# Second gather stage of a graph network: three tiles of each pair picked by TensorE, one comparison per five node blocks, targets loaded as a spread bf16 row

## The reference

```python
# layer 0: per relation r, sum of norm * h[src] into dst, times W_r = sum_b w_comp[r,b] weight[b]
x = layernorm(x + relu(segment_sum(...) @ W + h_bias + x @ loop_weight))
# layer 1, on the new x
e = (x[dst] - x[src]) @ theta.T + x[src] @ phi.T
e = relu(batchnorm(e, g0, b0))       # statistics over all edges
e = relu(batchnorm(e @ fc1.T, g1, b1))
x = layernorm(x + relu(segment_mean(e, dst) + x))
```

## Time and profile before

| what | us |
|---|---|
| median of three runs | 2537.24 |
| the profiled execution | 2537.5 |
| its span | 2535.7 |
| TensorE matmul busy | 2051.7 |
| GpSimd busy | 1562.5 |
| VectorE busy | 1546.1 |
| ScalarE busy | 652.8 |

### The profile page before, as it was taken

The page is one execution under the profiler, slowest core; times in us unless marked ns, Lnnn a source line. Parts: engine busy times, 40 slices in busy tenths (PEclk is TensorE's granted clock), DMA queues, the critical chain, the costliest instruction groups (busy, mean ns, idle before and its releaser), DMA issues. The chain is left out here.

```text
span 2535.7 us, 49004 instructions
## 1 busy us (share of the span) xinstructions
PE 2051.7 (81%) x13488; PEld 1691.6 (67%) x13489; DVE 1546.1 (61%) x4106; ACT 652.8 (26%) x1087; POOL 1562.5 (62%) x1715
## 2 busy tenths in 40 slices
PE   4777777777677677689888888988988998999996
PEld 3766666666667667546666666666665444999995
DVE  5443433434433344787867767777776787777776
ACT  3211111111111112541111111111111774444444
POOL 6777777777777775477777777777777001940002
PEclk9988888888888888759889989988988999999998
DMA  4222222222222221553434333343343993344442
GB/s 108 73 65 72 70 67 72 64 72 64 74 71 64 71 60 41 175 177 116 134 114 134 115 124 125 115 133 117 114 134 111 329 303 129 131 141 146 146 149 84
DMA packets 129354, 291.65 MB, mean 115 GB/s; under 512 B 34541, under 2 KB 83478, under 8 KB 111492
## 3 DMA queue, kind: packets, MB, share of 16 engines
q1 hardware_dynamic: 72532, 139.41, 17.1%
q0 software_dynamic: 48640, 99.61, 15.2%
q10 hardware_dynamic: 8112, 51.91, 5.2%
HBM read 227.59 MB, written 63.21 MB: 115 GB/s over the span
## 5 line engine op out<-in xcount | busy, mean ns | idle before, releaser
L759 POOL DMA_INDIRECT G<-in_x,srcT x782 | 744.3, 952 | 246.2 <-issue 180.4
L774 POOL DMA_INDIRECT G<-btab,srcT x738 | 696.3, 943 | 268.9 <-issue 167.6
L858 PE MATMUL PS<-BIG,G 128*128 128x192 f32 x1564 | 354.6, 379 | 258.6 <-PEq L36 257.6
L858 PEld LDWEIGHTS PS<-BIG,G 128*128 128x128 f32 x1564 | 297.2, 220 | 289.9 <-issue 289.4
L1145 ACT ACTIVATE BIG<-PS 128x768 f32<-128x768 f32 x196 | 158.5, 809 | 785.0 <-ACTq L36 784.6
L1460 DVE TENSOR_TENSOR ACC<-ACC,PS 128x24 f32 x782 | 140.8, 180 | 318.6 <-DVEq L36 228.1
L869 PE MATMUL PS<-BIG 128*128 128x192 f32 (+1 forms) x1584 | 329.5, 370 | 0.5 <-PEq L36 0.5
L869 PEld LDWEIGHTS PS<-BIG 128*128 128x128 f32 x1584 | 318.5, 227 | 0.6 <-issue 0.6
L987 PE MATMUL PS<-BIG,ACC 128*128 128x256 bf16 x2112 | 286.9, 297 | 24.8 <-PEq L36 24.7
L987 PEld LDWEIGHTS PS<-BIG,ACC 128*128 128x128 bf16 x2112 | 215.3, 106 | 96.1 <-issue 54.9
L1234 ACT ACTIVATE BIG<-PS 128x512 f32<-128x512 f32 x174 | 103.7, 596 | 594.4 <-ACTq L36 588.8
(11 more groups left out here) (208 smaller groups left out, 2347.6 us busy)
## 6 DMA issues: line engine op xcount, KB each, us to landing
BIG<-spill SPq DMA_DIRECT2D x90, 1024.0 KB, 4.9
spill<-BIG ACTq DMA_DIRECT2D x49, 1024.0 KB
G<-in_x,srcT POOLq DMA_INDIRECT x782
typ_i<-in_edge_type SPq DMA_DIRECT2D x97, 128.0 KB
G<-btab,srcT POOLq DMA_INDIRECT x738
BIG<-atab SPq DMA_DIRECT2D x196, 60.0 KB
atab<-BIG SPq DMA_DIRECT2D x12, 384.0 KB, 2.9
xn<-in_x SPq DMA_DIRECT2D x48, 64.0 KB
```

What stands on the lines that cost most here:

```text
L759: nc.gpsimd.indirect_dma_start(out=G[0:n, g % 2, t, :], out_offset=None, in_=x, in_offset=bass.IndirectOffsetOnAxis(ap=srcT[0:n, TPG * g + ...
L774: nc.gpsimd.indirect_dma_start(out=G[0:n, g % 2, t, :], out_offset=None, in_=btab[:, :], in_offset=bass.IndirectOffsetOnAxis(ap=srcT[0:n, ...
L858: mm = pe.matmul(PS[:, 2 * c + q // 2, (q % 2) * ZW:(q % 2 + 1) * ZW], G[:, h, TPC * k + q, :], soh[:, p, TPC * c + q, :, :].rearrange("p ...
```

## The change

- `PICK` becomes three tiles, so a pair has 29 gathers. The picking matmuls have 384 columns.
- The codes are written five times, the j-th lowered by j, so that one comparison with 5b makes the one-hots of the five blocks 5b to 5b+4 (`BATCH = 5`, ten batches, the last with four used blocks). The batches move: the first is made and used at chunk 0 of the pair.
- TensorE's spreading of picks and ScalarE's codes move ahead of chunk 0's own work on their engines.
- The targets are stored once in setup as bf16 rows in DRAM (`rel_d`, and as float32 in `relf_d` for chunks that span more than one window), and SyncE loads each group's row spread over 80 partitions. The spreading matmuls L973 go, and the look-up compares in SBUF. Its wait for the one-hot buffer (`cnt_done`) now stands in front of it.
- Four PSUM banks instead of two hold the chunks in work (`e_free` 4). The last chunk of a pair is copied in two activations.

```diff
-    PICK = 2 * TILE
-    PICK_Q = TPC - 2
+    PICK = 3 * TILE
+    PICK_Q = TPC - 3
-    PICK_ROW, PICK_COLS, PICK_STEP = 3, 86, 88
-    BATCH = 7
+    PICK_ROW, PICK_COLS, PICK_STEP = 3, TILE, TILE + 2
+    BATCH = 5
+    NBATCH = 10
...
-            return {1: (0,), 2: (1,), 3: (2,), 4: (3,), 5: (4,), 6: (5, 6)}.get(at_c, ())
+            return {0: (0,), 1: (1, 2), 2: (3,), 3: (4, 5), 4: (6,), 5: (7, 8), 6: (9,)}.get(at_c, ())
...
                 take(sp, dig_free)
-                sp.dma_start(digits[:, h, :], digits_d[:, bass.ds(g * GROUP, GROUP)]).then_inc(dig_in[h], 16)
+                row = rel_d[bass.ds(g * CPG, CPG), :].rearrange("(o k) n -> o (k n)", o=1).to_broadcast([WIN, CPG * REL_CHUNK])
+                sp.dma_start(rel[:, h, :, :].rearrange("p k n -> p (k n)"), row).then_inc(dig_in[h], 16)
...
                     for k in range(CPG):
                         if wide_chunks:
                             reach = reach_of(pe, CPG * g + k)
+                        if picking(g, h, use) and h == 0 and k == 0:
+                            spread_picks()
                         reached(pe, "pe", b_gathered[CPG * h + k], b_landed(g, h, use, k))
...
-                        nxt = after(g, h, use, k)
-                        nxt = nxt and after(*nxt)
-                        if nxt:
-                            spread_dst(*nxt)
...
             def code_picks():
                 take(act, pick_spread_done)
                 act.sem_inc(pick_rows_free, 1)
-                full = PICK // PICK_COLS
-                act.activation(pick_code[:, 0:full, 0:PICK_COLS], pick_spread[:, 0:full * PICK_COLS].rearrange("p (r c) -> p r c", r=full),
-                               ACT.Identity, bias=small[:, 62:63])
-                act.activation(pick_code[:, full, 0:PICK - full * PICK_COLS], pick_spread[:, full * PICK_COLS:PICK],
-                               ACT.Identity, bias=small[:, 62:63]).then_inc(pick_code_ready, 1)
+                for j in range(BATCH):
+                    ins = act.activation(pick_code[:, j, :, 0:PICK_COLS], pick_spread.rearrange("p (r c) -> p r c", r=PICK_ROW),
+                                         ACT.Identity, bias=pick_bias[:, j:j + 1])
+                ins.then_inc(pick_code_ready, 1)
...
                     if u is not None:
                         unit_high_part(u)
+                    if picking(g, h, use) and h == 0 and k == 0:
+                        code_picks()
                     take(act, look_done)
...
                     if u is not None:
                         unit_mid_part(u)
-                    if picking(g, h, use) and h == 0 and k == 0:
-                        code_picks()
                 act.sem_inc(dig_free, 1)
...
-            def look_up(k):
-                take(dve, d_ready)
-                dve.tensor_scalar(ohT[0:WIN, k % 2, :], PS[0:WIN, k % 2, :], node_col[0:WIN, 0:1], None, ALU.is_equal).then_inc(ohT_ready, 1)
+            def look_up(g, h, use, k):
+                if k == 0:
+                    reached(dve, "dve", dig_in[h], 16 * (use + 1))
+                dve.tensor_scalar(ohT[0:WIN, k % 2, 0:CHUNK + 1].rearrange("p (r n) -> p r n", r=REL_ROW),
+                                  rel[:, h, k, :].rearrange("p (r n) -> p r n", r=REL_ROW)[:, :, 0:REL_COLS],
+                                  node_col[0:WIN, 0:1], None, ALU.is_equal).then_inc(ohT_ready, 1)
...
-                for w in range(BATCH * b, BATCH * (b + 1)):
-                    ins = dve.tensor_scalar(pick_oh[:, BATCH * (b % 2) + w % BATCH, :].rearrange("p (r c) -> p r c", r=PICK_ROW),
-                                            pick_code[:, :, 0:PICK_COLS], float(w), None, ALU.is_equal)
-                ins.then_inc(pick_oh_ready, 1)
+                take(dve, pick_oh_free)
+                dve.tensor_scalar(pick_oh[:, BATCH * (b % 2):BATCH * (b % 2 + 1), :].rearrange("p j (r c) -> p (j r) c", r=PICK_ROW),
+                                  pick_code[:, :, :, 0:PICK_COLS].rearrange("p j r c -> p (j r) c"), float(BATCH * b), None,
+                                  ALU.is_equal).then_inc(pick_oh_ready, 1)
```

More of the change, by code:

```diff
@@ L197, in gnn_kernel @@
         awx = part(3 * D // 2).bitcast(BF16).rearrange("p (a d) -> p a d", a=3)
+        relx = part(CHUNK)[0:WIN, :]
+        pick_hi, pick_rows = (part(PICK // 2).bitcast(BF16) for _ in range(2))
         at[0] = 2 * GROUP + CPG * CHUNK + GROUP
@@ L236, in gnn_kernel @@
         f_hi, f_lo, f_dst, f_min = (rows(accf, k) for k in range(4))
-        i_rel, i_hi = (rows(accf, k, I32) for k in range(4, 6))
+        i_hi = rows(accf, 5, I32)
         a_hi = i_hi
-        dig_hi, dig_lo = (bst[0:NR, k, :].bitcast(BF16).rearrange("p (b e) -> p b e", b=TPR) for k in range(2))
+        rel_rows_b = flat(bst[:, :, :])[0:NR, 0:TPR // TPC * REL_CHUNK // 2].bitcast(BF16).rearrange("p (c r n) -> p c r n", c=TPR // TPC, r=REL_ROW)
         t_min, t_max, t_first, t_reach, t_ext = (part(TPR)[0:NR, :] for _ in range(5))
@@ L670, in store_picks @@
                 sp.wait_ge(picks_ready, 1)
-                for k, dg in enumerate((pick_lo64, pick_hi)):
+                for k, dg in enumerate((pick_lo, pick_hi)):
                     sp.dma_start(picks_d[k, :, :], dg[0:ODD, :]).then_inc(rows_out, 16)
@@ L984, in pick_rows_of @@
                 take(pe, pick_oh_ready)
-                for w in range(BATCH * b, BATCH * (b + 1)):
+                for w in range(BATCH * b, min(BATCH * (b + 1), NW)):
                     for a in range(3):
-                        mm = pe.matmul(picked, table_part(w, a), pick_oh[:, BATCH * (b % 2) + w % BATCH, 0:PICK],
+                        mm = pe.matmul(picked, table_part(w, a), pick_oh[:, BATCH * (b % 2) + w % BATCH, :],
                                        start=(w == 0 and a == 0), stop=False, skip_group_check=True)
@@ L1137, in copy_z @@
             def copy_z(g, h, use):
+                if isinstance(g, int) and g == 1:
+                    act.wait_ge(rows_out, 16 * 6)
                 for k in range(CPG):
@@ L1233, in store_e @@
                     else:
-                        act.activation(to, PS[:, 2 + k % 2, :], ACT.Copy).then_inc(act_self, 1)
+                        act.activation(to, PS[:, k, :], ACT.Copy).then_inc(act_self, 1)
                         take(act, act_self)
@@ L1604, in count_hots @@
                 tiles = bass.ds(TPG * g + TPC * k, TPC)
-                take(dve, cnt_done)
                 dve.tensor_tensor(oh_lo[:, k % 2, :, :], over(steps_lo, TPC, TNODES), each(loT[:, tiles], TNODES), ALU.is_equal)
@@ L1681, in one @@
                         if nxt:
-                            look_up(nxt[3])
+                            take(dve, cnt_done)
+                            look_up(*nxt)
                             count_hots(nxt[0], nxt[3])
                         u = unit_of(g, k)
-                        if u is not None:
-                            unit_rest_part(u)
                         if isinstance(g, int) and (g, k) == (1, 1):
@@ L1701, in one @@
                             dve.sem_inc(look_done, 1)
+                        if u is not None:
+                            unit_rest_part(u)
                         if k >= 1:
@@ L1712, in edge_features @@
                 by_pairs(dve, NG, one, head=FIRST_PICK, tail=HELD // 2)
-            look_up(0)
+            look_up(0, 0, 0, 0)
+            take(dve, cnt_done)
             count_hots(0, 0)
```

71 lines of the change are left out of this document (33 added, 38 removed).

## The result

| | before | after |
|---|---|---|
| median, us | 2537.32 (6 runs, 2535.61 to 2538.57) | 2615.45 (6 runs, 2613.41 to 2616.12) |
| ratio to before | | 1.0306 (95%: 1.0293 to 1.032) |
| span of the profiled execution, us | 2535.7 | 2613.8 |
| last count of the second gather stage | 1962.67 | 2041.45 |

The change costs 78 us. All of it is in the one stage: its last count comes 78.8 us later. The forecast was 2634 us, with a mechanism, a loop through three engines, of 41.8 us a pair; the pair is 40.96 us.

A forecast was written before the change was run, and what follows sets the result against it. Gathers bound the stage before; afterwards a three-engine loop: 33.0 + 6.5 = 39.5 us plus 2.3 low clock, 41.8 a pair, ending the stage 97.5 us later: 2537 + 97 = 2634 us, range 2550 to 2662 (own range 2610 to 2660).

The forecast's parts named there:

- chunks 1 to 6: TensorE's work on six chunks of a pair, without picking matmuls: 1.35 us each, 8.1 us of the loop.
- last chunk: TensorE's part of the pair's last chunk in the loop: one transpose 0.11, look-up 0.65, its end 0.17; 0.9 us.
- last look-up to batch 0: From TensorE's last look-up through ScalarE's copy, spill and codes and VectorE's comparison to the first picking matmuls: 6.5 us.
- low clock on the loop: TensorE at half clock behind its idle time, no longer hidden by gathers: 2.3 us a pair, bounds 1.5 and 3.2.
- pair: Period of one pair of groups in the gather stage: loop 39.5 us plus low clock 2.3, so 41.8 us.
- first batch 0; end: Stage's first picking batch at 1139.1 us; its end at 1140.6 + 22 P, P the pair's period: 2060.2 us.
- What becomes last: the loop: Chain through TensorE, ScalarE and VectorE from batch 0 to the next: 39.5 us against 36.2 for the gathers.
- rival 1: Same loop, but TensorE's clock stays up or falls in few pairs: 39.5 us a pair, 2584 us; chance 0.20.
- the chunk without spreading: TensorE's chunk without picking, once the eight target-spreading matmuls go: from 1.60 to about 1.35 us.
- Rival 2: Gathers stay last because codes are ready in time and TensorE's wait costs nothing: 27.4 us less, 2510 us; chance 0.11.
- Rival 3: New VectorE comparisons and look-ups run in two-port mode and stretch gathers: 41.4 us a pair, 2623 us; chance 0.03.
- the targets' row: DMA on SyncE's queue bringing targets to 80 partitions, 330 KB per group in place of 8 KB: taken as nothing.

The follow-up runs named there:

- early: Changed kernel with only the order moved: next pair's pick spreading, codes and first comparison made earlier, same work; 2529.49 us, ratio 0.9969.
- filled: Changed kernel plus 60 unused 128-column matmuls on TensorE behind chunk 0 of each pair, where it idled; 2563.98 us, ratio 1.0104.
- one_code: Changed kernel where ScalarE makes all five code rows only for the first picking pair and one for each later pair; 2580.97 us, ratio 1.0172.
- early_codes: Changed kernel with only the spreading of the next pair's picks and their codes moved ahead, first comparison left in place; 2597.33 us, ratio 1.0236.
- early2: The order of early, with the second batch's comparison also made one chunk sooner; 2509.1 us, ratio 0.9884.
- two_tiles: Changed kernel selecting two tiles per pair (256 columns) instead of three, the third gathered again, codes in ten rows of 128; 2573.52 us, ratio 1.0136.
- thin_rows: Changed kernel with the targets' row spread to 8 partitions instead of 80 from the third group on; 2614.24 us, ratio 1.0305.

## Why the prediction was right, and where its numbers were off

| step, as predicted | predicted | measured |
|---|---|---|
| gather, from start to start | 1.248 us, then waits for buffers | 944 ns + 0.30; waits to 4.0 |
| picking matmul of 384 columns | 0.163 us | 0.163 (30 in 5.04 less 15 in 2.60) |
| chunks 1 to 6 | 6 x 1.35 = 8.1 us | 6 x 1.20 = 7.2 |
| last chunk | 0.9 us | 0.94 |
| look-up 513 columns | 0.41 us | 0.475 |
| codes, comparison | 2.5, 1.15 us | 2.46, 1.146 |
| last look-up to batch 0 | 6.5 us | 6.6 |
| low clock on the loop | 2.3 us | 2.3 |
| pair | 41.8 us | 40.96 |
| first batch 0; end | 1139.1; 1140.6 + 22 P | 1138.70; 2041.45 (by the formula 2041.7) |

- **What becomes last: the loop.** Shown by early: the same instructions in another order take 86 us less. Its length came from rows of before because each of its links was there already, one chunk away from being late.
- **The clock.** The choice between the forecast and rival 1 (2584) rested on today's 4.67 us of idle time ahead of every low stretch. TensorE's idle time came out at 4.9, and the low stretch with it in every pair; filled shows its price, 51 us. The size of 2.3 us a pair came out; the reason given for it, a low stretch whose place shifts from pair to pair, did not show here: batch 0 takes 4.96 us in 18 of the 21 turns and 4.79 to 4.94 in the first three. So that the size fits is in part luck. A shifting place showed in one_code, early_codes and early.
- **The term that was mis-sized** is the chunk without spreading: 1.35 instead of 1.20. The earlier trace rows has 0.20 us from the counts to the spreading and 0.32 from there to the picking. I took 0.25 of these 0.52 away; in the new chunk counts to picking is 0.11, so 0.41 go (1.60 to 1.19). 0.15 x 6 = 0.9 us a pair is the whole gap between 41.8 and 40.96, and 22 x 0.84 = 18.5 us the gap between 2634 and 2615.
- **Rival 2** (gathers last, 2510) was wrong as a forecast of this order and right as the value of another: early2 takes 2509.1. The prediction's condition, codes and comparison off the path, is what early2 fulfils.
- **Rival 3** (two-port comparisons). The argument against it was the 0.944 beside comparisons of three rows by 86, and the shape rows-in, run-out. It held, but for a reason it did not name: the number of rows is odd in both. Rows in and run out was not enough: two_tiles kept that shape with ten rows, and its gathers grew. Thirty rows cost early2 3.2 us of gathers a pair (69.5 / 22). In the changed kernel that would have made 39.4 of them, an estimate, still under the loop of 41.
- **Costed at nothing and nothing it was:** the targets' row (thin_rows).

## What to carry to other kernels

Sum the loads of the engines, and then also walk once around every chain that returns to its start within one turn of the loop. Here all engines had room (TensorE 33.6 of 36.2 us by load, 147 x 0.163 + 8 x 1.20) and one link that moved a chunk forward closed a loop of 41 us. Such a loop is undone by order, at no cost in work: make the next turn's inputs a chunk before they are due, and move all the paths that meet in the same instruction, since moving one of two nearly equal ones gives little (18 of 106 us here). And where gathers are the bound, look at the shape of VectorE's copies and comparisons between SBUF tiles: a faster mode can cost more than it saves.

## What the runs showed of the hardware that was not expected

- The mode of a VectorE comparison of two-byte data follows the number of rows: 1280 columns take 505 ns on average as ten rows (0.47 to 0.49 us where no gather holds the comparison up) and 812 as five; 1920 take 672 as thirty rows (on average; 0.65 us in the timeline) and 1146 as fifteen.
- A gather beside the fast form can be stretched by most of the form's duration (944 ns to 1.50 us beside 0.65 us; 0.32 us for each comparison on average), beside the slow form not at all (944 and 945 ns). It goes the other way too: a fast comparison begun 0.55 us into a gather takes 0.71 us instead of 0.49 (two_tiles, at 1519.25). The Trainium skill (SBUF — State Buffer, "SBUF: two separate sides") calls the shared ports an exclusive lock that whoever starts first holds for the whole instruction. That each side can hold up the other agrees with it. That a gather holds the lock for its whole duration does not: the comparison at 1526.55 begins 0.07 us into a gather and neither is longer, and the one at 1519.25 would have ended at 1520.12 or later had it waited for the gather's end at 1519.64, and ended at 1519.96.
- 60 matmuls without use, put into an idle stretch of TensorE, took 51 us off the time: the stretch behind it ran at 2.4 GHz instead of 1.2.
- The clock fell behind waits much shorter than the 4.67 us of before as well, but not each time: behind 3.70 us the 15 matmuls took 4.96 us in some turns and 3.92 in others (one_code), behind 1.76 us the 30 matmuls took 6.71 us in seven of 20 turns (early), and behind 1.55 us, with the 60 matmuls ahead of them, it did not fall (filled, 15 matmuls in 2.60 us).
